# GpSimd in a cross-attention kernel: a copy for a product by one, and two products with a scalar per row for one product of two tensors

## The reference, cut to what matters

```python
x = x + xattn(layernorm(x), ctx)      # 8 heads of 64, 112 queries, 375 keys
x = x + ffn(layernorm(x))             # 8 experts, 2 per token, and a shared expert
```

```python
q = (x @ Wq).reshape(b, n, 8, 64); k = (ctx @ Wk)...; v = (ctx @ Wv)...
sim = einsum('bihd,bjhd->bhij', q, k) * 64 ** -0.5
attn = softmax(sim, axis=-1)
out = einsum('bhij,bjhd->bihd', attn, v).reshape(b, n, 512) @ Wout + bout
```

## Time and profile before

| What | Value |
|---|---|
| Runs | 1150.12, 1144.87, 1144.96 us |
| Median | 1144.96 us |
| Profiled execution, its span from first to last instruction | 1154.2 us |
| Its own time beside the span | none recorded; the span stands for it |
| Mean granted TensorE clock | 0.986 of full speed |
| `attention` | about the first 687 us |
| One pair in the loop | 40.09 us |
| Busy, TensorE / VectorE / ScalarE / GpSimd | 95% / 66% / 60% / 60% |

### The profile page before, as it was taken

The page is one execution under the profiler, slowest core; times in us unless marked ns, Lnnn a source line. Parts: engine busy times, 40 slices in busy tenths (PEclk is TensorE's granted clock), DMA queues, the critical chain, the costliest instruction groups (busy, mean ns, idle before and its releaser), DMA issues. The chain is left out here.

```text
span 1154.2 us, 26175 instructions
## 1 busy us (share of the span) xinstructions
PE 1097.8 (95%) x7534; PEld 967.9 (84%) x7534; DVE 766.7 (66%) x2024; ACT 691.0 (60%) x1667; POOL 694.4 (60%) x629
## 2 busy tenths in 40 slices
PE   5989999999999999999999889999999999999996
PEld 4778888888888888888888779999888888888886
DVE  4778888888888888888888756675633333333332
ACT  4777777777777777777777754542233443443332
POOL 3797778768777877787787745665223333333333
PEclk9999999999999999999999998989999999999999
DMA  5223143133214322331342339222465336333861
GB/s 150 82 59 97 57 132 103 56 106 120 89 57 131 109 71 85 125 99 49 123 139 70 118 119 339 92 73 87 134 200 136 55 56 162 57 58 58 258 173 15
DMA packets 103698, 124.04 MB, mean 107 GB/s; under 512 B 19712, under 2 KB 71888, under 8 KB 103632
## 3 DMA queue, kind: packets, MB, share of 16 engines
q1 hardware_dynamic: 83376, 99.82, 26.6%
q0 software_dynamic: 11760, 15.15, 7.4%
q10 hardware_dynamic: 8496, 8.22, 2.5%
HBM read 74.40 MB, written 49.68 MB: 108 GB/s over the span
## 5 line engine op out<-in xcount | busy, mean ns | idle before, releaser
L520 POOL TENSOR_TENSOR probs<-probs,inv_sum 112x750 f32<-112x750 f32 x128 | 183.8, 1437 | 134.5 <-DVE inv_sum L974 134.4
L1726 POOL DMA_INDIRECT out<-stage,to_row x48 | 74.9, 1559 | 173.5 <-ACT stage L1778 125.2
L2006 DVE TENSOR_TENSOR hT_lo<-banks,hT_hi 128x512 fp32r<-128x512 f32 x63 | 43.6, 691 | 184.5 <-ACT hT_hi L1770 178.6
L690 ACT ACTIVATE probs<-banks,neg_max 112x375 f32<-112x375 f32 x256 | 145.9, 573 | 18.3 <-DVE neg_max L961 15.4
L961 DVE TENSOR_REDUCE neg_max<-banks 112x2 f32<-112x750 f32 x128 | 119.8, 936 | 47.7 <-PE banks L1320 46.0
L487 POOL TENSOR_TENSOR v_both<-v_raw,v_both 125x512 fp32r<-125x512 f32 x96 | 123.2, 1284 | 7.5
L1346 PE MATMUL banks<-ident,probs 112*125 112x112 f32 x768 | 106.9, 275 | 12.7 <-DVE pT L967 12.7
L1334 PE MATMUL banks<-pT,v_both 125*128 125x224 f32 x768 | 114.0, 284 | 5.1 <-DVE oT_lo L992 5.0
L1334 PEld LDWEIGHTS banks<-pT,v_both 125*128 125x128 f32 x768 | 99.2, 192 | 23.2 <-issue 21.4
L967 DVE TENSOR_TENSOR pT<-banks,pT 125x672 fp32r<-125x672 f32 x128 | 108.6, 849 | 14.4 <-ACT pT L681 13.1
L1346 PEld LDWEIGHTS banks<-ident,probs 112*125 112x125 f32 x768 | 97.0, 189 | 24.1 <-issue 20.0
(11 more groups left out here) (292 smaller groups left out, 3206.0 us busy)
## 6 DMA issues: line engine op xcount, KB each, us to landing
w_split_scratch<-stage SPq DMA_DIRECT2D x16, 1536.0 KB, 8.2
ring<-w_split_scratch SPq DMA_DIRECT2D x16, 1536.0 KB
stage<-in_L_ffn_W SPq DMA_DIRECT2D x48, 256.0 KB, 2.9
ctx_in<-in_ctx SPq DMA_DIRECT2D x32, 281.2 KB
xg<-x_sorted_scratch ACTq DMA_DIRECT2D x59, 136.0 KB
x_in<-in_x SPq DMA_DIRECT2D x16, 224.0 KB, 2.5
x_res<-in_x SPq DMA_DIRECT2D x32, 112.0 KB, 2.1
x_scratch<-x SPq DMA_DIRECT2D x32, 112.0 KB, 1.9
```

What stands on the lines that cost most here:

```text
L520: pool.tensor_tensor(probs[:, two, :], probs[:, two, :], inv_sum[:, 2 * s:2 * s + 2].rearrange("p (e o) -> p e o", o=1).to_broadcast([N, 2 ...
L690: act.activation(probs[:, h % 4, :], S_BANKS[0:N, e, 0:M], ACT.Exp, bias=neg_max[:, h:h + 1], accum_out=row_sum[:, h:h + 1]).then_inc(exp_ ...
```

## The change

Two instructions of GpSimd are written otherwise; nothing else is touched. The product by `one` becomes a `tensor_copy` with the same input and output. The product of `probs` (112 rows of two heads times 375) with `inv_sum` spread along the row becomes two `tensor_scalar` products, one for each head, with one scalar per row. The wait that stood on each of these instructions now stands on an instruction of its own that raises a new semaphore which nobody waits for.

```diff
+        raw_seen, inverse_seen = sem("raw_seen"), sem("inverse_seen")
...
                 pool.wait_ge(unit_hi, n_hi)
+                pool.sem_inc(raw_seen, 1)
                 raw = v_raw[at_v][:].rearrange("p (h d) -> p h d", h=HEADS)
-                pool.tensor_tensor(v_both[b][:, t, :, 0, :], raw,
-                                   one[0:KR, :].rearrange("p (o q) -> p o q", o=1).to_broadcast([KR, HEADS, DH]),
-                                   ALU.mult).then_inc(v_hi_ready, 1)
+                pool.tensor_copy(v_both[b][:, t, :, 0, :], raw).then_inc(v_hi_ready, 1)
                 pool.wait_ge(v_hi_ready, n_v)
...
                 pool.wait_ge(inv_ready, 8 * p + s + 1)
-                pool.tensor_tensor(probs[:, two, :], probs[:, two, :],
-                                   inv_sum[:, 2 * s:2 * s + 2].rearrange("p (e o) -> p e o", o=1).to_broadcast([N, 2, M]),
-                                   ALU.mult).then_inc(probs_ready, 1)
+                pool.sem_inc(inverse_seen, 1)
+                for e in range(2):
+                    row = probs[:, two.start + e, :]
+                    last = pool.tensor_scalar(row, row, inv_sum[:, 2 * s + e:2 * s + e + 1], None, ALU.mult)
+                last.then_inc(probs_ready, 1)
```

## The result

The changed kernel takes **1167.34 us** (median of 4 runs, 1164.06 to 1169.13) against 1144.91 us for the kernel before (4 runs, 1144.83 to 1150.12): ratio 1.0179, 95% interval 1.0153 to 1.0206. It is 1.8% slower, which is clear of the noise; the medians lie 22.4 us apart, and the ratio makes 20.5 us. The forecast of 1144.7 us and its range both missed, and so did the sign.

A forecast was written before the change was run, and what follows sets the result against it. TensorE was taken to bound the kernel, setting each loop pair's length. The terms summed to 14 x 0 in the loop and -0.3 us near the last pair, giving 1144.7 us, range 1140.8 to 1151.5.

The forecast's parts named there:

- The scaling: GpSimd's probability scaling, 8 in a pair: from 1.437 us to two products of 0.54 us, 1.08 us together.
- By the nearest kind: Scaling rate taken from two affine selects and a 4-element tensor-scalar product: 0.90 ns an element, 1.08 us for two.
- The upper bound of 0.99 us: Most that one row product on GpSimd should take, from a two-tensor subtraction at 2.13 ns an element; 1.99 us for two.
- The copy: GpSimd's copy in place of the product by one, 6 in a pair: from 1.042 to 0.66 us, bounds 0.59 and 1.04.
- The moved waits: Waits on instructions of their own on GpSimd, 14 in a pair: 0.05 us each, ends 0 and 0.1.
- The cover: Loop slack between GpSimd's scaling and TensorE's transpose: 1.31 us at the least against at most 0.65 us more, so nothing felt.
- the second view: Busy time by stretch: in a 40.09 us pair TensorE has 39.21 us of work, GpSimd 31.11, with 9 us to spare.
- If that cover were gone, five times a pair: In the loop, each microsecond of scaling past the slack would be paid up to five times a pair.
- The rival for slower: Slow row scalar: from 1.37 us a product it shows; at 1.6 us GpSimd becomes the bound, 43 us lost, 1188 us; chance 0.05.
- The last pair: Scaling of step 7, weight split, store, load, ScalarE near 638 us: 0.31 us won, bounds 0.58 won to 0.65 lost.
- VectorE gains: Shorter GpSimd instructions let VectorE's low part come sooner: up to 12.3 us won, 1132.7 us, half 1138.8; chance 0.04.
- Two clock stretches: Clock rival: two low-clock stretches fewer, 3.5 us, give 1141.2 us; chance past 0.5% 0.04 up, 0.04 down.

The follow-up runs named there:

- 12: Changed kernel with a second operation, times 1.0, on each row product: 1142.12 us in one run (kernel before: 1147.97).
- 17: Changed kernel with a second operation, times 1.0, and each head's product cut into 188 and 187 elements: 1162.00 us (kernel before: 1160.12).
- experiment 3: Kernel before with only the two waits moved to instructions of their own: 1147.34 us in one run (kernel before: 1148.73).
- experiment 1: Changed kernel with the old scaling, one product of two tensors, put back; copy and moved waits kept: ratio 0.9998 to the kernel before.
- experiment 10: Changed kernel with the row products only in the first and last pair, the 14 loop pairs with the old product: ratio 1.0067 to the kernel before.
- experiment 8: Changed kernel with two products of two tensors, one a head, in place of the row products: 1150.31 us (kernel before: 1148.06).
- experiment 2: Changed kernel with the product by one put back for the copy, row products kept: ratio 1.0395 to the kernel before.
- experiment 13: Kernel before with copy and moved waits, plus an unread 128 x 512 GpSimd subtraction behind each scaling: ratio 1.0032 to the kernel before.

## Why the prediction was wrong, by its own steps

**The scaling: the term that failed.** "By the nearest kind" I took 0.90 ns an element from the two affine selects and the 203 ns of L1653. Experiments 12 and 17 show 0.85 ns an element and 0.27 us fixed, so the rate was right, for a form that the change does not use: L1653 carries two operations, the new line one. The trace did hold one row of the one-operation form, which I passed over (L1659, 128 x 4 elements, 234 ns for L1653's 203), but at 4 elements it can show no rate:

```profile
L1659 POOL TENSOR_SCALAR nbias<-nbias 128x4 f32<-128x4 f32 x6 | 1.4, 234 | 0.5
```

The upper bound of 0.99 us was the real error: it assumed that one input can't cost more per element than two. The runs show 2.5 ns against 1.66, and against the 2.13 of the bound. The term was 8 x (1.08 + 0.05 - 1.44) = -2.5 us a pair and measured 8 x (2.46 - 1.44) = +8.2.

The Trainium skill's GPSIMD Engine Reference, section on engine selection, puts one-input work at roughly line rate; by the page's clock of 1.2 GHz that is an estimated 0.83 ns an element. The two-operation form, with 0.85 ns, comes near to that; the one-operation form, with 2.5 ns, is three times off it, and the measurement decides.

**The copy: right. The moved waits: half of what they cost.** The copy takes 0.61 to 0.63 us for 0.66. A moved wait delays the scaling by 0.10 us for 0.05, the upper end of the range (experiment 3); the cover hides it, and the time shows neither (experiments 1 and 3).

**The cover: the second step that failed.** "1.31 us at the least", and so a rival that "decides from 1.37 us each". At 1.24 us each the step grew by 1.02 us, which is less than 1.31, and by that reckoning the loop would have stayed at 40.09. It didn't, and not at steps 5 and 4. Slack between a scaling and its transpose is a snapshot with GpSimd on time. Longer steps make the next start late as well, and in a queue without idle time this adds up: step 2 had 1.5 us of slack, its scaling starts 1.06 us later in the pair (4.70 for 3.64 us) and takes 1.02 longer, so 0.6 us are lacking. By the last table the loop gives way between 2.18 and 2.33 us for a step, so at 1.09 to 1.17 us a product, not at 1.37. I had the second view in hand, 9 us of spare time in a pair, but not where it lies; of the change's remaining 4 us, 3.5 stand before steps 4 and 5.

**"If that cover were gone, five times a pair": too much.** It is 2.4 times near the edge. TensorE waits at two steps, and the wait at step 1 takes the place of the 0.63 us for VectorE's low part.

**The rival for slower: right in sign, wrong in mechanism.** It had 0.05. GpSimd did not become the bound (36.8 of 40.8 us busy), the scalar was not at fault, and the price was 22 us instead of 43.

**The last pair: the right chain, the wrong sign and size.** I named one place on the path and gave it -0.3 us. The chain is there (ScalarE waits 5.16 us for its load, 2.48 before), but it was not the only one: TensorE waits 2.53 us for GpSimd at step 0, and the two ends together carry 7.7 us (5 to 10 by the interval of experiment 10). The slack table that I made for all 128 steps had it: in the last pair steps 0, 5 and 7 had 0.41, 0.75 and 0.61 us, and I quoted the loop's values alone. Of the last pair's own 2.7 us the clock can account for all: 53.30 x 0.87 = 46.4 and 50.60 x 0.93 = 47.1 us are estimates of it at the full clock. The granted clock is 0.63 in the four us after TensorE's wait of 2.53 us, and 0.50, the 1.2 GHz level, from 668. The wait is not needed for a lower clock: experiment 8 has none there, and its last pair takes 53.3 us at 0.90. What brings the lower clock, and how the 7.7 us of the ends divide further, stays open.

**VectorE gains: not seen, but the rival looked at the wrong instruction.** VectorE's low part takes 849 ns in both kernels. Its layer-norm instruction (`xn`, L862) does depend on GpSimd: it takes 0.40 us by itself and up to 1.37 us in the kernel before, where it ends 0.15 us after the GpSimd instruction beside it. In experiment 1 none of the 32 is held (0.40 to 0.41), and the reciprocals of step 2 come 0.3 us sooner; the pair is 40.06 all the same, so there was nothing to gain in the loop.

**Small slips that change nothing.** Two clock stretches of 1.7 us are 3.4 and not 3.5; the ends of the range, 1140.8 and 1151.5, follow from no sum that is shown; and in the fifteenth pair the slack of step 7 is 4.3 and not 3.0 us.

## What to carry to other kernels

Price an instruction by its exact form, the number of its operations included, at two sizes before it is swapped in, and let the bound for an unmeasured form reach past the forms that look heavier. For an engine that works through a queue, cover is not the slack of one instruction: follow the queue from its last idle time on, add up what each step gains in length, and compare the sum with the slack of every step behind it, at the ends of the program too. An engine that is busy for 90% of a stage can stall the bounding one, though not the bound itself; and a saving on it that is worth nothing now (the copy, ratio 0.9998) is worth some 25 us as soon as something else makes it late (0.0395 - 0.0179 of 1149 us, experiment 2 against the change). Look also at what the engine next to it does while it runs longer: here VectorE's reciprocals moved with GpSimd's timing.

## What the hardware showed that was not expected

- On GpSimd a tensor-scalar instruction with one operation takes 0.3 us and 2.5 ns an element (375 elements: 1.24 us; an addition 1.24, with a constant 1.17); with a second operation, times 1.0, it takes 0.27 us and 0.85 ns (0.59 us). The product of two tensors lies between, 1.66 ns. Why the shorter program is the slower one stays open.
- With the quick form the last pair's granted clock is 1.00 and it takes 47.2 to 47.4 us, for 0.93 and 50.6 us before, in two profiles on two chips. A scaling 0.25 us shorter a step gives nothing in the loop and 3 us there. It does not go by the scaling alone: the last pair takes 53.2 to 53.3 us at 0.90 with scalings of 1.63 and 1.73 us (experiments 8 and 17), and 50.0 us at 0.91 with 2.48 (experiment 2).
- A VectorE tensor-scalar instruction from SBUF to SBUF (112 x 256) takes 0.40 to 0.41 us when nothing holds it. Beside a GpSimd instruction it took up to 1.49 us: of 576 over all traces 232 took longer than 0.43 us, and 215 of these end 0.15 us after a GpSimd instruction does. VectorE's low part, which reads PSUM and one SBUF tensor, takes 0.83 to 0.86 us in all 128 cases of the kernel before and of experiment 13.
- A wait moved from a GpSimd instruction to a semaphore instruction of its own ahead of it delays the start by 0.10 us (0.18 for 0.08).
